# A hybrid of attention, state-space layer and routed experts: the state-space part one step later, taps and decay sums in odd steps, the mask folded into the decay product

## The chip, the cores and the metric

The kernel runs on one core of a Trainium2 chip. The metric is the device time of one execution in microseconds. A core has TensorE (PE; PEld is its weight load), VectorE (DVE), ScalarE (ACT), GpSimd (POOL) and SyncE (SP, here only DMAs). Each engine takes its instructions strictly in the order in which they are written and waits for semaphores in between.

## The reference, cut to what matters

Input x is (8, 32, 32, 128), so 8 images of 1024 tokens with 128 channels.

```python
q = (x * dw1) @ pw1 + b1;  v = (x * dw2) @ pw2 + b2       # per image, 1024 tokens
a = softmax(q @ q.T) @ v * gamma + x                       # attention, no scaling
t = a
n = layernorm(t); xn = rmsnorm(n) * norm_w
z, xBC, dt = split(xn @ W_in.T)                            # 256, 320, 8
xBC = silu(causal_conv4(xBC) + conv_b)                     # four taps
xs, B, C = split(xBC);  dt = softplus(dt + dt_bias)
state = state * exp(-dt * exp(A_log)) + (dt * xs) outer B  # along the tokens, 8 heads of 32, 32 states
y = C . state + Dp * xs
y = rmsnorm(y * silu(z)) * gnorm_w
t = t + n + y @ W_out.T
m = layernorm(t); p = top2(softmax(m @ router_w.T))        # 8 experts, gates sum to 1
out = t + sum over the two of gate * (silu(m @ w1.T) * (m @ w3.T)) @ w2.T   # hidden size 341
```

## The kernel before, in words

The 8192 tokens are 64 tiles of 128. A batch is 8 tiles, one image. `batches` calls `step(base, i)` 79 times; `base` is the batch's first tile and i runs from 0 to 7. The calls are unrolled, and each engine has its own `step` with an order written out by hand. What a step holds:

- tile base+i: its scores against the whole image (TensorE L339 to L341, into pX), their row maximum NM (VectorE L976) and their exponential PR (ScalarE L610). Q is kept as a high and a low part, QH and QL, so that three products of a fast type give full precision.
- tile o = i-1: PR is transposed (L329, into pY), copied to PT (ScalarE L579), multiplied with V (L423, into pa), and TA = product x 1/sum x gamma + X (VectorE L1050).
- every second step, for two tiles at once: the norms of TA (GpSimd L845 to L851), XN and its transposes (odd steps, tiles i-3 and i-2, "front a"), the products for z, dt, x, B and C. In even steps ("front b", tiles i-4 and i-3) VectorE does SZ (L981), softplus of dt (dts, L985 to L1030, a chain of small instructions) and the other three taps of the convolution (`conv`, L950, nine instructions). The first term is ScalarE's CV (L643, three activations).
- tile k = i-LAG, LAG = 5: the state-space part. In odd steps, for two tiles ("decays"), VectorE makes SX (L955) out of Tanh of the taps (TH, ScalarE L663), reads the running sums of dt x A out of bank pc (CT), and splits them into three bf16 parts (C3), which TensorE transposes (L372) and ScalarE copies to CT3 and NCT3. Each tile has its transposes of SX (L378, L379), the exponents of the decay between every two tokens, in pY (L390, L391, L393), their exponential ED (ScalarE L622), M = ED x GT (VectorE L1041), XDT (L1009), XW (GpSimd L811), and the new state ST (L1098).
- tile e = i-LAG-1: y of the tile (L362, L366, into pc), Y2 (VectorE L997 or L999), YG = Y2 x silu(z) (GpSimd L805), its transposes (L403), the output product (L428), and T2 (VectorE L1056).

The exponent product adds three terms per pair of tokens: `later`, a 128x128 bf16 matrix with -1e30 where a token would look ahead (L390), minus the sum at one token (L391) and plus the sum at the other (L393).

At batch ends there is more. In step 7 TensorE makes the Q of the next batch (`project_q`), and in step 0 V (`project_v`), to which GpSimd adds b2 (L855). For the batch before: GpSimd computes the experts' norm at the end of step 5 (L773 to L777), ScalarE the normalised rows XA in step 6 (L653), TensorE their transposes and the logits through bank pd in step 7 (L306, L312). For the batch before that, VectorE runs `route_a` (softmax, best two, one-hot) in step 1 and `route_b` (a row's place in its expert's list) in the middle of step 3, and GpSimd scatters 16 blocks of rows to DRAM in steps 3 to 7 (L858). Behind the last step comes a table of which expert each block of 128 rows belongs to. Then 136 such blocks go through the experts (L496 to L524, L867), and the results are added to T2 and stored.

Two orders matter for the change. ScalarE, even step:

```python
A(TZ[:, j, :], (pb, pd)[j][:, 0:DI], ACT.Tanh)   # L595, twice
A(dts[:, 2], dts[:, 1], ACT.Exp)                 # L597
A(BNAT[:], pa[:, 2 * P:3 * P], ACT.Copy)         # L603, then GT, PR, SQ, YT, XNT, ED
```

VectorE, even step: three taps, NM, SZ and dts, Y2, two of the softplus chain, XDT, the rest of the chain with three taps in between, AD, M, TA, T2, three taps, CT, YO, ST.

## Time and profile before

| | |
|---|---|
| median of 3 runs | 1317.82 us (1317.07 to 1322.14) |
| the profiled execution | 1313.46 us, of which the span is 1311.5 us |
| TensorE busy | 1128.5 us, 86% of the span |
| VectorE | 908.1 us, 69% |
| ScalarE | 689.1 us, 53% |
| GpSimd | 603.7 us, 46% |
| attention with the state-space part | from 16 to some 895 us of the span |
| end of routing, table, last scatters | to 950 us |
| experts | to 1263 us |
| sum and store | to 1311.5 us |

An engine's busy time is the sum of its instructions' time without overlap. Matmul ends are modelled, so neighbouring ones overlap on paper; the distance from start to start tells what one costs.

### The profile page before, as it was taken

What the parts mean: (1) busy time and instruction counts of PE and PEld (TensorE: products, weight loads), DVE (VectorE), ACT (ScalarE), POOL (GpSimd) and SP (SyncE); (2) the same over time, 40 slices, a digit from 0 to 9 for tenths busy, and PEclk for the clock granted to TensorE, in tenths of its full rate; (3) what the DMA queues carried; (4) which work ended last, traced back from release to release, by engine and by line L of the source; (5) the groups of instructions that cost most, each with busy time, mean ns of one, the idle gap of its engine ahead of it and who ended that gap; (6) DMA issues with size and microseconds to landing.
All of it is one profiled execution on the core that took longest, in us unless ns stands there. A gap on an engine that the chain in (4) does not pass through costs nothing. (4 is left out here: it accounts for less than half of the span.)

```text
span 1311.5 us, 28238 instructions
## 1 busy us (share of the span) xinstructions
PE 1128.5 (86%) x7681; PEld 949.8 (72%) x7745; DVE 908.1 (69%) x3041; ACT 689.1 (53%) x1748; POOL 603.7 (46%) x846
## 2 busy tenths in 40 slices
PE   4799999999999999899999999873099999999950
PEld 3688888788778878788878877752078888888740
DVE  2578778978987987987997988672445555555534
ACT  2565676576666666566657656532034444444420
POOL 5133333483475375466458347435434444444420
PEclk9899999999999999999999999886599999999985
DMA  6000000010010010010010100000112222222249
GB/s 180 26 1 9 25 2 9 20 35 14 5 46 17 1 44 16 9 40 20 9 36 22 27 8 20 10 5 29 53 51 58 58 58 57 58 58 58 56 112 301
DMA packets 73029, 54.66 MB, mean 42 GB/s; under 512 B 9781, under 2 KB 67677, under 8 KB 72925
## 3 DMA queue, kind: packets, MB, share of 16 engines
q1 hardware_dynamic: 55437, 31.62, 9.0%
q0 software_dynamic: 8448, 17.45, 4.0%
q10 hardware_dynamic: 9040, 4.33, 1.1%
q8 instruction: 50, 0.82, 0.3%
q14 instruction: 54, 0.44, 0.1%
HBM read 30.67 MB, written 22.69 MB: 41 GB/s over the span
## 5 line engine op out<-in xcount | busy, mean ns | idle before, releaser
L867 POOL DMA_INDIRECT results_by_choice<-YE,DIX x136 | 130.6, 960 | 190.3 <-ACT YE L698 181.1
L858 POOL DMA_INDIRECT rows_by_expert<-XA,SL x128 | 139.2, 1088 | 63.9 <-issue 31.9
L1176 DVE COPY V<-pc 128x384 f32<-128x384 f32 x136 | 75.9, 558 | 132.7 <-PE pc L516 132.7
L362 PEld LDWEIGHTS pc<-XDT,M 128*128 128x128 f32 x1024 | 125.3, 196 | 35.6 <-issue 30.3
L362 PE MATMUL pc<-XDT,M 128*128 128x64 f32 x1024 | 126.4, 278 | 23.1 <-DVE CT L1081 10.5
L950 DVE SCALAR_TENSOR_TENSOR CV<-XBC,cw,CV 128x256 f32<-128x256 f32 x288 | 131.2, 490 | 9.8 <-ACT CV L643 3.2
L423 PE MATMUL pa<-V,PT 128*128 128x128 f32 x1024 | 126.8, 277 | 2.2 <-POOL V L855 0.9
L423 PEld LDWEIGHTS pa<-V,PT 128*128 128x128 f32 x1024 | 119.4, 192 | 6.6 <-issue 6.3
L507 PE MATMUL pX<-W,TA 128*128 x272 | 104.3, 464 | 1.0 <-ACT TA L685 0.7
L509 PE MATMUL pY<-W,TA 128*128 x272 | 101.1, 454 | 0.0
L1041 DVE TENSOR_TENSOR M<-ED,GT 128x1024 f32<-128x1024 f32 x64 | 78.3, 1224 | 32.8 <-ACT ED L622 32.8
L805 POOL TENSOR_TENSOR YG<-Y,SZ 128x256 f32<-128x256 f32 x64 | 46.6, 727 | 108.1 <-DVE Y L997 97.5
L1172 DVE TENSOR_TENSOR X<-XT,pY 128x341 f32<-128x341 f32 x136 | 69.5, 511 | 31.5 <-PE pY L509 19.5
L796 POOL TENSOR_TENSOR STE<-ST,ETOT 32x256 f32<-32x256 f32 x56 | 46.6, 831 | 91.9 <-DVE ST L1098 87.8
L976 DVE TENSOR_REDUCE NM<-pX 128x1 f32<-128x1024 f32 x64 | 77.8, 1216 | 14.3 <-PE pX L341 14.1
L663 ACT ACTIVATE TH<-CV 128x768 f32<-128x768 f32 x32 | 27.0, 844 | 114.8 <-issue 101.8
L685 ACT ACTIVATE TA<-pa 128x128 f32<-128x128 f32 x136 | 37.8, 278 | 79.6 <-PE pa L496 78.7
L610 ACT ACTIVATE PR<-pX,NM 128x1024 f32<-128x1024 f32 x64 | 71.3, 1115 | 9.4 <-DVE NM L976 9.4
L329 PE MATMUL pY<-ident,PR 128*128 128x128 f32 x512 | 68.2, 277 | 3.5 <-ACT XBC L638 2.7
L516 PE MATMUL pc<-ident,X 128*128 128x128 f32 (+1 forms) x408 | 66.9, 273 | 0.0
L524 PEld LDWEIGHTS pb<-W,V 128*128 128x128 f32 (+1 forms) x408 | 56.1, 191 | 14.0 <-issue 1.1
L329 PEld LDWEIGHTS pY<-ident,PR 128*128 128x128 f32 x512 | 57.9, 146 | 11.5 <-issue 10.5
(252 smaller groups left out, 3023.0 us busy)
## 6 DMA issues: line engine op xcount, KB each, us to landing
GX<-rows_by_expert SPq DMA_DIRECT2D x136, 65.0 KB
XT<-in_xT_dram SPq DMA_DIRECT2D x8, 512.0 KB, 3.9
X<-in_x_dram SPq DMA_DIRECT2D x16, 256.0 KB, 3.0
W<-results_by_choice SPq DMA_DIRECT2D x8, 512.0 KB, 8.6
out_dram<-T ACTq DMA_DIRECT2D x8, 512.0 KB, 6.8
results_by_choice<-YE,DIX POOLq DMA_INDIRECT x136, 2.2
rows_by_expert<-XA,SL POOLq DMA_INDIRECT x128
W<-in_w1T_dram SPq DMA_DIRECT2D x1, 1364.0 KB
```

What stands on the lines that cost most here:

```text
L329: last = nc.tensor.transpose(pY[:, P * j:P * j + P], PR[:, P * j:P * j + P], ident[:])
L362: mm(pc[:, 64 * h:64 * h + 64], M[:, h, :], XDT[:, e % 2, HD * h:HD * h + 64], start=h == 0, stop=False, skip_group_check=True)
L423: last = mm(pa[:, 0:C], PT[:, P * j:P * j + P], V[:, j, :], start=j == 0, stop=j == NT - 1)
L507: mm(pX[:, 512 * par:512 * par + HID], GXT[:, par, :], W1[:, cols], start=True, stop=True).then_inc(s("h1_ps"), 1)
L509: mm(pY[:, 512 * par:512 * par + HID], GXT[:, par, :], W3[:, cols], start=True, stop=True).then_inc(s("h3_ps"), 1)
L610: A(PR[:], pX[:], ACT.Exp, bias=NM[:, i:i + 1], accum_out=RS[:, i:i + 1]).then_inc(s("exp_ready"), 1)
L858: g.indirect_dma_start(xg, bass.IndirectOffsetOnAxis(ap=SL[:, j // NT, j % NT:j % NT + 1], axis=0), XA[:, j // NT, j % NT, :], None).then_ ...
L867: g.indirect_dma_start(yg, bass.IndirectOffsetOnAxis(ap=DIX[:, j, :], axis=0), YE[:, j, :], None).then_inc(s(f"ye{j}_scattered"), 16)
L950: return stt(CV[:, m, :], XBC[:, m, fo + tap:fo + tap + 256], cw[:, m, tap:tap + 1], CV[:, m, :], ALU.mult, ALU.add)
L976: v.tensor_reduce(NM[:, i:i + 1], pX[:], AX.X, ALU.max, negate=True).then_inc(s("nm_ready"), 1)
L1041: tt(M[:], ED[:], GT[:, None, :].broadcast_to([P, H, P]), ALU.mult).then_inc(s("m_ready"), 1)
L1176: v.tensor_copy(HT[:, par].rearrange("p k t -> p (k t)"), pc[:, 0:P * len(HC)]).then_inc(s("hT_ready"), 1)
```

## The change

The state-space part runs a step later (LAG 6), while the decay sums stay at i-5 (called d now) and are applied, with the taps, in odd steps. SX and CTP move to the start of the even steps. SZ gets a third buffer.

The mask goes into the product with NCT3. Rows 64 to 127 of NCT3 hold -1e30 where a token would look ahead, once for each half of the tokens, and `pickm` picks them:

```diff
-  mm(pY[:, q], identb[:], later[:, None, :].broadcast_to([P, 4, P]), start=True, stop=False, ...)
-  mm(pY[:, q], NCT3[:, par, :], pick[:, half * H + 4 * h2:half * H + 4 * h2 + 4, :], start=False, ...)
+  four = pY[:, 512 * h2:512 * h2 + 512].rearrange("p (h t) -> p h t", h=4)
+  for th in range(2):
+      mm(four[:, :, HP * th:HP * th + HP], NCT3[:, par, th, :], pickm[:, half * H + 4 * h2:half * H + 4 * h2 + 4, :], start=th == 0, ...)
```

VectorE's `step`, cut to its order (i even: SX; i odd: decay sums and taps):

```diff
-                if decays:
-                    stt(SX...)                      # needs TH
-                    v.tensor_copy(C3[:, 0], CUM) ... # the C3 chain
-                if front_b:
-                    conv(2, 0); conv(2, 1); conv(2, 2)
+                if i % 2 == 0 and there(base, k):
+                    upto(dve, "th_ready", base, k + 2)
+                    stt(SX...)
+                if decays:
+                    upto(dve, "cum_ps", base, d + 2)
+                    tt(CT..., pc[:, 0:4 * H]..., hrow[:, 1:2, :]..., ALU.mult)   # CT = sums x -A
+                    upto(dve, "cv_evac", base, d + 2)
+                    conv(2, 0)
+                    ... C3 chain with conv(2, 1) and conv(2, 2) in between
                 if there(base, i):
                     v.tensor_reduce(NM...)
+                if i == 1 and routes:
+                    routing[base] = route_a(base)
+                    route_on()                      # softmax of the logits, up to PB / sum
...
                 Y2, recip and two small ones of softplus (three now)
                 XDT
+                if decays:
+                    conv(1, 0); conv(1, 1); conv(1, 2)
-                if i == 1 and there(base, -2 * NT): route_a(base)
-                if i == 3 and there(base, -2 * NT): route_b(base)
                 softplus chain, RG            # no taps in between any more
+                if i in (1, 2) and routes: route_on()
+                if decays:
+                    conv(0, 0); conv(0, 1); conv(0, 2)    # then conv_ready
                 M, TA, T2, the two statistics
+                if i in (2, 4) and there(base, NT): take_ql(base + NT, [i // 4])
                 YO, ST
+                if i in (1, 2) and routes: route_on()
+                if i == 2 and routes: PCT copy
+                if i == 3 and routes: route_b(base)
+                if i == 0 and routes: logits copy, maximum, subtraction
```

`route_a` is a generator now, in four parts: softmax; maxima; indices and one-hots; gates. The first two parts and the third run in step 1 (ahead of Y2, ahead of the last three taps, at the end), the fourth in step 2.

ScalarE, even step: TR of two tiles and PT first, then CTP, the two TZ, and now CV ahead of the exponential of dts; in step 0 four of the batch's normalised rows (`normed(base, 1)`) behind it:

```diff
                 if front_b:
                     ... TZ, twice
+                    for m in range(3):
+                        last = A(CV[:, m, :], XBC[:, m, fo:fo + 256], ACT.Identity, bias=cb[:, m:m + 1], scale=cw[:, m, 3:4])
+                    last.then_inc(s("cv_evac"), 2)
                     A(dts[:, 2], dts[:, 1], ACT.Exp).then_inc(s("enau_ready"), 2)
+                if routes:
+                    normed(base, 1)
```

ScalarE, odd step: the exponential of the logits (i = 1) behind XN; TH behind ED and ahead of the two XBC copies, where it stood at the end of the even step. The first four normalised rows come at the end of step 7 (they were eight, in step 6).

TensorE: `project_q` one half in step 2 and one in step 4 into a second buffer of QH and QL, where it was whole in step 7; transposes of the normalised rows and the logits in step 0 of the next batch, in bank pc (`rows_of_x(base, 0)` behind L403, `rows_of_x(base, 1)` behind `project_v`, `logits` behind the state products), where they were in step 7 in bank pd; logits 8 columns wide instead of 64; the sums of dt (not of dt x A) over 16 columns instead of 64.

GpSimd: V isn't biased; b2 x gamma is added to X instead, a half in step 7 and a half in step 3 (`bias_x`, 128x512 each). The experts' norm moves from the end of step 5 to the end of step 6, behind that step's four scatters and norm chain. Its setup builds `pickm` and the masked NCT3, and ScalarE waits for them before its first step.

SyncE: the padding rows go to a DRAM tensor early and from there to their places, the loads of x wait for constants. ZT shares XA's memory. V, the expert stage and the table aren't changed.

## Rows read from the trace of the kernel before

**Rows 1.** Busy time by stretch: from:to, length, each engine's busy time, clock, DMA.

```profile
89.90:192.30 102.40, 97.89 (x720) 85.13 (x727) 80.08 (x248) 68.31 (x167) 37.26 (x68) 1.00 0.04 12
812.70:895.00 82.30, 63.48 (x415) 52.98 (x418) 55.36 (x207) 35.28 (x94) 38.34 (x57) 0.88 0.04 12
```

**Rows 2.** The same for steps 0, 2 and 4 to 7 of one batch: PE, PEld, DVE, ACT, POOL.

```profile
405.54:418.49 12.95, 12.90 (x102) 11.81 (x102) 11.79 (x38) 7.48 (x16) 2.77 (x5) 1.00 0.01 2
...
431.54:444.40 12.86, 12.04 (x89) 10.38 (x90) 12.00 (x39) 7.35 (x16) 3.73 (x5) 1.00 0.01 3
...
457.25:469.96 12.71, 11.68 (x85) 9.90 (x86) 11.49 (x38) 6.58 (x15) 7.94 (x10) 1.00 0.06 18
469.96:482.69 12.73, 11.66 (x85) 9.71 (x86) 9.03 (x27) 8.69 (x24) 8.96 (x14) 1.00 0.24 84
482.69:494.49 11.80, 11.22 (x85) 9.95 (x86) 10.88 (x35) 9.01 (x22) 10.00 (x13) 1.00 0.05 18
494.49:511.53 17.04, 16.12 (x115) 13.52 (x116) 11.58 (x34) 11.65 (x30) 12.81 (x17) 1.00 0.07 25
```

**Rows 3.** TensorE in order of time, steps 4 to 6: start, length, instruction, wait.

```profile
465.14 0.44 PE L403 MATMUL pb<-ident,YG 128*128 128x128 f32 x2 [0.42 <-POOL YG L805]
465.67 2.02 PE L423 MATMUL pa<-V,PT 128*128 128x128 f32 x16
...
469.47 0.43 PE L480 MATMUL pc<-AD,tri 128*128 128x64 f32 x2 [0.46 <-DVE AD L1036]
...
477.87 0.39 PE L403 MATMUL pb<-ident,YG 128*128 128x128 f32 x2
...
482.69 1.06 PE L329 MATMUL pY<-ident,PR 128*128 128x128 f32 x8 [0.25 <-ACT XBC L638]
...
488.66 0.81 PE L390 MATMUL pY<-later,identb 128*128 128x512 bf16 x2
...
489.52 0.61 PE L393 MATMUL pY<-CT,pick 128*128 128x128 bf16 x8
```

**Rows 4.** ScalarE in order of time, steps 4 and 5.

```profile
457.13 1.59 ACT L643 ACTIVATE CV<-XBC,cb,cw 128x256 f32<-128x256 f32 x3
...
460.66 0.39 ACT L595 ACTIVATE TZ<-pd 128x256 f32<-128x256 f32 x1
...
463.36 0.22 ACT L597 ACTIVATE dts<-dts 128x16 f32<-128x16 f32 x1 [2.32 <-DVE dts L985]
...
472.56 0.84 ACT L663 ACTIVATE TH<-CV 128x768 f32<-128x768 f32 x1 [5.65 <-issue]
...
474.61 0.41 ACT L573 ACTIVATE CTP<-SX 32x256 f32<-32x256 f32 x1 [1.00 <-DVE SX L955]
...
476.39 0.88 ACT L589 ACTIVATE XN<-TA,st 128x128 f32<-128x128 f32 x2
```

**Rows 5.** VectorE in order of time, step 4.

```profile
463.85 0.43 DVE L997 TENSOR_TENSOR Y<-pc,YO 128x256 f32<-128x256 f32 x1
```

**Rows 6.** GpSimd in order of time, step 6.

```profile
483.90 1.34 POOL L773 TENSOR_SCALAR rs<-MV 128x8 f32<-128x8 f32 x1 [0.16 <-issue]
...
488.81 0.73 POOL L805 TENSOR_TENSOR YG<-Y,SZ 128x256 f32<-128x256 f32 x1 [0.49 <-DVE Y L999]
...
500.31 0.20 POOL L851 TENSOR_TENSOR st<-st 128x4 f32<-128x4 f32 x1
```

**Rows 7.** VectorE in order of time, first and last part of `route_b`.

```profile
918.95 1.57 DVE L926 TENSOR_TENSOR OFF<-OFF,PCT 128x8 f32<-128x8 f32 x8
...
922.58 0.17 DVE L933 CAST SL<-SLF 128x16 uint32<-128x16 f32 x1 [0.24 <-DVE SLF L932]
```

**Rows 8.** VectorE and GpSimd in order of time, a tap and XW.

```profile
385.00 0.94 DVE L950 SCALAR_TENSOR_TENSOR CV<-XBC,cw,CV 128x256 f32<-128x256 f32 x1
385.02 0.63 POOL L811 TENSOR_TENSOR XW<-XDT,DEC 128x256 f32<-128x256 f32 x1
```

**Rows 9.** The page's costliest groups: count, busy us, mean ns, idle before.

```profile
L950 DVE SCALAR_TENSOR_TENSOR CV<-XBC,cw,CV 128x256 f32<-128x256 f32 x288 | 131.2, 490 | 9.8 <-ACT CV L643 3.2
```

More of the change, by code:

```diff
@@ L729, in _ @@
             g.memset(cb[:], 0.0).then_inc(s("zeroed"), 1)
[L730 to L731 removed]
+            for t, v in ((wx[:, DI + 2 * NS:], 0.0), (CTP[:], 0.0), (XBC[:, :, 0:TAPS - 1], 0.0), (CT3[:], 0.0),
+                         (ST[:], 0.0), (XDT[:, :, DI:], 0.0), (ones[:], 1.0), (mhalf[:], -0.5)):
                 g.memset(t, v)
             g.memset(tri[:], 1.0)
[L734 removed]
             g.memset(pick[:], 0.0).then_inc(s("filled"), 1)
@@ L833, in step @@
                 scatters(3)
-                if i == 5 and there(base, -NT) and not last_norm:
-                    norm_for_experts(base)
                 if i % 2 == 0 and there(base, fn):
@@ L1004, in step @@
                     steps.then(tt(dts[:, 5], dts[:, 2], dts[:, 9], ALU.mult))
+                    steps.then(tt(dts[:, 6], dts[:, 5], dts[:, 5], ALU.mult))
                 if there(base, k):
@@ L1034, in step @@
                 if front_b:
-                    upto(dve, "cum_ps", base, fb)
-                    stt(AD[:, 0:16].rearrange("p (a b) -> p a b", a=2), DT[:, fpar], -1.0, hrow[:, 1:2, :].broadcast_to([P, 2, H]), ALU.mult, ALU.mult).then_inc(s("ad_ready"), 2)
+                    steps.then(stt(DT[:, fpar], dts[:, 7], 2.0, dts[:, 3], ALU.mult, ALU.add), True)
+                    v.nop().then_inc(s("dt_ready"), 2)
+                if i in (1, 2) and routes:
+                    route_on()
+                if decays:
+                    upto(dve, "conv_tap1", base, d + 2)
+                    for m in range(3):
+                        last = conv(0, m)
+                    last.then_inc(s("conv_ready"), 2)
                 if there(base, k):
```

441 lines of the change are left out of this document (222 added, 219 removed).

## The prediction

> **What bounds the kernel now.** I read the page first, then busy time by stretch, then one batch step by step, then one even and one odd step on each engine. In the long stretches [rows 1] the reader is to see TensorE busy for about 96% of a batch at full granted clock (1.00), and VectorE 85% beside it. The eight steps of one batch last 511.53 - 405.54 = 105.99 us [rows 2]. Every step but the last takes 11.8 to 13.05 us (step 1 from the ends of its neighbours); the last takes 17.04, because the Q product and the router's transposes and logits stand in it. So the attention stage is TensorE's, with a few small waits: 0.42 us for YG, 0.46 for AD, 0.25 for the XBC copy [rows 3]. VectorE is busy 9.0 to 12.0 us of each step shown [rows 2]; it has the least room in the even ones. Whatever makes a TensorE instruction wait lengthens the step at once, since each engine runs in its written order and TensorE has nothing in hand to catch up with.
>
> **Work removed from TensorE.** The decay mask was two bf16 products of 512 columns with `later` beside two with `pick`: 489.52 - 488.66 = 0.86 us for the four [rows 3]. Now four products of 256 columns do both, at the same rate 0.43 us. That is 0.43 saved per tile, 3.4 us per batch and 27.5 us over 64 tiles. The narrower decay sums and logits save nothing that I count: they keep their number of weight loads. The Q product (two products, 1.72 us) moves from step 7 into steps 2 and 4, and transposes with logits (about 2.6 us) from step 7 to the next step 0; together they are the 4.3 us by which step 7 exceeds step 5 [rows 2]. Both only move.
>
> **Even steps.** ScalarE now makes the taps' first term CV (three activations, 1.59 us) between the second TZ and the exponential of dts [rows 4]. The second TZ starts 460.66 - 457.25 = 3.4 us into the step, so that exponential starts at 3.4 + 0.4 + 1.5 = 5.3 (now 6.1, held there by VectorE). From it to Y2 are 463.85 - 463.36 = 0.5, and from Y2 to the transposes of YG (L403) 465.14 - 463.85 = 1.3 [rows 3 to 5]: L403 at 7.1. By its own order TensorE would be there at 489.52 - 482.69 = 6.8, plus about 0.45 for the products with CT3, less 0.43: 6.85. L423 waits for XDT, which stands 465.67 - 463.85 = 1.8 behind Y2, and 0.2 more for the square of dts put ahead of it: 7.9. Behind L423 come 469.96 - 465.67 - 0.46 = 3.8 us (the wait for AD goes, as the taps leave the even step). An undisturbed even step is 11.7 us, against 11.80 for step 6. The 0.43 saved is spent waiting for YG and XDT.
>
> **Odd steps.** They gain the nine tap instructions on VectorE (131.2 / 288 = 0.46 us each, 4.1 us [rows 9]) and lose SX (1.0, the wait of CTP [rows 4]). Of step 5 TensorE is idle 12.73 - 11.66 = 1.07 us [rows 2]; most of that is the wait of L362 for CT, about 0.7, and it goes. Its work is 11.66 - 0.43 = 11.2 us. But Tanh of the taps (TH, 0.84 [rows 4]) now needs the last tap and stands on ScalarE ahead of the two XBC copies, and the next step's first transposes already wait for the second of these [rows 3]. L403 of an odd step is at 477.87 - 469.96 = 7.9 today [rows 3], less 0.7 and 0.43: 6.8. XDT starts about there, six taps and two small instructions (3.2) end near 10.1, TH 11.0, the copies 11.9: I take 12.0 us. A clean pair is then 23.7 us, against 24.5 for steps 5 and 6.
>
> Taps against GpSimd: one tap took 0.94 us, where the mean is 0.49, when XW started beside it [rows 8, 9]. Between 0 and 0.5 us per odd step come from that; 0.1 is in the 12.0. The Trainium skill (SBUF — State Buffer, "Who interferes with whom") has it that a VectorE instruction with two SBUF inputs and a GpSimd instruction that reads SBUF shut each other out for a whole instruction. By that rule every odd step, with three taps right behind XDT just as XW is released, pays up to the whole 0.5; the sum would be some 14 us higher. The row agrees that it happens, not how often.
>
> **What the new order does to the routing steps** (six batches route in the attention loop, two behind it).
> Step 1: four small router instructions stand on VectorE ahead of Y2 and wait for ScalarE's exponential of the logits, behind XN. XN stood at 476.39 - 469.96 = 6.4, now some 0.7 earlier; with 0.9 for XN, 0.3 for PB and 1.0 for the four, Y2 is at 7.9, L403 at 9.2, where TensorE would be at 6.8. With the 482.69 - 477.87 = 4.8 us from L403 to the end of an odd step: 14.0.
> Step 2: the maxima's indices and one-hots (some 2 us) run behind step 1 on VectorE, which then is 3.2 us late; SX, CTP, TZ, CV, dts, Y2 follow one on another: L423 at 9.3, plus 3.8, 0.86 and 0.4 for the places: 14.3.
> Step 3: 12.0. Its router block of 922.75 - 918.95 = 3.8 us [rows 7] now stands at the very end, ahead of step 4's SX. VectorE is 5.2 late: SX to CTP 1.0, CTP 0.35, two TZ 0.9, CV 1.5 (the exponential starts near 8.8), then 0.5 and 1.3: L403 near 10.6 instead of 6.85, L423 11.2. Step 4, with its half of Q: 11.2 + 3.8 + 0.9 = 15.9.
> Steps 5 and 6: 12.0 and 11.7.
> Step 7: GpSimd normalises for the experts at the end of step 6, behind four scatters and the norm chain. Today that norm chain ends 500.51 - 488.81 = 11.7 us behind the start of YG of step 6. The experts' chain with STE takes 488.81 - 0.49 - 483.90 = 4.4, of which some 1.1 is its first instruction held up (1.34 instead of about 0.2) [rows 6]: 3.3. YG of step 6 starts at 6.4, so step 7's can't start before 6.4 + 11.7 + 3.3 - 11.7 = 9.7, where 5.2 would do. L403 at 10.4, plus 4.8: 15.2; I take 15.0.
> Step 0: 11.7, V 1.8, transposes and logits 2.6, and 0.4 because ScalarE enters late (it normalises four tiles at the end of step 7, four here): 16.5.
> Sum 16.5 + 14.0 + 14.3 + 12.0 + 15.9 + 12.0 + 11.7 + 15.0 = 111.4 us, against 105.99: 5.4 more. Waits worked out like these partly cover each other, so I take 4.9, 29 us over six batches.
>
> **The rest.** Batch 1 routes nothing: four pairs, Q and V (3.5) and 1.7 in step 7 make 99.5 against 102.40 [rows 1]: -3. Batch 0 holds one state-space tile less and needs no biased V (about -7), while Q's halves sit in steps of only 5 us (+2): -5. Behind attention one more state-space step is needed, 7 to 12 us; the 82.30 us there [rows 1] stand mostly for VectorE, which is better spread, and the experts' norm no longer waits for a scatter: between -4 and +9, I take +3. V's bias on X costs GpSimd 2.4 us per batch as before, hidden in steps 7 and 3. The zero rows go by a DRAM tensor; their eight DMAs stay beside 16 scatters: 0, at most 3. The expert stage isn't touched.
> Sum: 29 - 3 - 5 + 3 = +24 us on the profiled execution's 1313.46. Its span was 1311.5, so 2 us lie around it; the median of the runs shown is 4.4 above it. 1317.8 + 24 = 1342; I say 1340.
>
> **Rivals.**
> (a) TensorE stays the bound (faster). The lags on VectorE and GpSimd are absorbed, because the taps' removal leaves even steps slack: this decides if step 4's L403 starts before 8 us and step 7's before 7.5. Then a batch is 105.99 - 3.4 = 102.6, today's waits included; six batches -20, with the rest -5: 1293. For it: steps now run with VectorE 3 us late and hardly stall. Against it: the instructions between were few; now SX, CV and Y2 form one row.
> (b) Only one of the two long waits comes (step 4 or step 7), about 3 us less per batch: 1321, within the noise. For it: GpSimd's scatters vary from 1.0 to 2.1 us.
> (c) The change doesn't remove what it says: the mask saving is eaten as above but no wait is added: 106 per batch, near 1314.
>
> **How the numbers follow.** Forecast 0.58, (a) 0.28, (b) and (c) 0.14 together. About 0.5% is what a measurement of this kernel can tell from no change. Faster 0.29, same 0.13, slower 0.58. Forecast alone: 1326 to 1360 (the open taps' term, and waits that cover each other). The whole range, which takes in most of (a): 1288 to 1358.
>
> **What would show it.** L403's waits for YG in steps 1, 4 and 7 of over 2 us each; VectorE starting SX of step 4 some 5 us into it; norm for experts ending 6 us or more into step 7; L390 gone and L391's four products near 0.43 us; no wait for AD or CT. If step 4 lasts under 13.5 us and step 7 under 13, I am wrong and the kernel is faster.

## The result, and the profile after

The changed kernel takes 1380.22 us (median of 4 runs, 1375.06 to 1383.37) against 1317.44 us before: ratio 1.0467, 95% interval [1.0425, 1.0509]. It is slower, as forecast, but by 63 us where 24 were forecast, and above the whole range of 1288 to 1358. Its profiled execution took 1379.51 us with a span of 1377.7 us, 66.2 us more than before's 1311.5.

Steps here begin at the first transposes of PR. One routing batch of the kernel after, steps 0 to 7, in the columns of [rows 2] (last: granted clock, DMA share, GB/s):

```profile
421.72:437.62 15.90, 15.57 (x126) 14.40 (x126) 11.69 (x34) 12.19 (x29) 7.70 (x14) 1.00 0.17 58
437.62:454.35 16.73, 14.55 (x88) 13.13 (x88) 11.62 (x43) 8.27 (x22) 2.74 (x5) 0.80 0.00 1
454.35:468.12 13.77, 12.27 (x92) 10.86 (x92) 12.07 (x55) 8.87 (x20) 2.71 (x5) 1.00 0.01 2
468.12:480.23 12.11, 11.81 (x89) 10.30 (x88) 10.84 (x32) 7.99 (x22) 5.62 (x11) 1.00 0.01 1
480.23:498.33 18.10, 13.71 (x88) 11.82 (x88) 15.24 (x51) 8.29 (x19) 9.84 (x11) 0.91 0.10 31
498.33:510.20 11.87, 11.51 (x89) 10.22 (x88) 10.33 (x29) 7.76 (x21) 8.98 (x15) 1.00 0.05 18
510.20:521.06 10.86, 10.55 (x83) 9.66 (x84) 8.99 (x29) 7.63 (x18) 4.34 (x7) 1.00 0.06 21
521.06:539.48 18.42, 14.46 (x89) 12.93 (x88) 12.18 (x34) 8.24 (x21) 15.81 (x23) 0.81 0.07 23
```

The reader is to see three things. Undisturbed steps (5 and 6) are shorter than before, together 22.73 us against 24.53 [rows 2]. Steps 1, 4 and 7 are long, and TensorE is idle in them for 2.2 to 4.4 us. And just these three have a granted clock under 1.00 (1.00 is 2.4 GHz, 0.50 is 1.2). The idle time is the forecast wait for YG at its transposes (L405, before L403), TensorE in order of time:

```profile
447.83 0.33 PE L405 MATMUL pb<-ident,YG 128*128 128x128 f32 x1 [2.18 <-POOL YG L823]
...
491.54 0.33 PE L405 MATMUL pb<-ident,YG 128*128 128x128 f32 x1 [3.52 <-POOL YG L823]
...
531.71 0.48 PE L405 MATMUL pb<-ident,YG 128*128 128x128 f32 x1 [3.73 <-POOL YG L823]
```

Against [rows 3], where the wait was 0.42 us. What the forecast did not have is in finer windows of steps 4 and 7:

```profile
490.00:492.00 2.00, 0.44 (x2) 0.20 (x2) 1.90 (x7) 1.93 (x7) 0.95 (x2) 1.00 0.00 0
492.00:494.00 2.00, 1.72 (x13) 1.75 (x14) 1.81 (x9) 1.31 (x3) 1.58 (x2) 0.84 0.03 8
494.00:496.00 2.00, 2.00 (x10) 2.00 (x10) 1.50 (x3) 0.00 (x0) 1.72 (x3) 0.50 0.11 33
...
532.00:534.00 2.00, 2.00 (x11) 2.00 (x10) 1.09 (x2) 1.66 (x5) 1.80 (x3) 0.50 0.11 33
534.00:536.00 2.00, 2.00 (x11) 2.00 (x11) 1.23 (x1) 0.95 (x2) 1.84 (x3) 0.50 0.10 33
```

Behind the wait TensorE is busy all the time, but at 0.50. The sixteen products of L425 in step 4 take 2.76 us (2.02 in [rows 3]):

```profile
492.29 2.76 PE L425 MATMUL pa<-V,PT 128*128 128x128 f32 x16 [0.31 <-issue]
```

The same wait does not always do it. Of the 18 waits in steps 1, 4 and 7 of the six routing batches, 17 have such a stretch behind them. The one without is in step 4 of batch 6 (counted from 0), where TensorE waited 3.23 us; that step lasted 16.2 us, where the five others lasted 17.8 to 18.7:

```profile
712.42:728.59 16.17, 12.07 (x88) 10.47 (x88) 14.61 (x49) 8.29 (x19) 8.49 (x10) 1.00 0.04 13
```

And some such stretches stand behind no wait. In step 1 of two batches, this one included, the clock is at 0.50 from 1.1 us into the step, before the wait for YG, although TensorE had been busy without a break (V's products, the router's transposes, sixteen products of 8 columns):

```profile
430.00:437.62 7.62, 7.62 (x64) 7.29 (x65) 4.61 (x16) 3.97 (x9) 3.45 (x10) 1.00 0.30 104
438.80:442.20 3.40, 3.40 (x13) 2.91 (x12) 2.87 (x11) 1.45 (x4) 0.00 (x0) 0.50 0.00 0
```

These two steps lasted 16.7 us, the four others 15.1. What brings this stretch no run here isolates.

Over the whole kernel, L425 (L423 before), L405's wait and the taps, against [rows 9]; the tap's mean rose from 490 to 555 ns, 18 us in all:

```profile
L425 PE MATMUL pa<-V,PT 128*128 128x128 f32 x1024 | 151.8, 310 | 11.6 <-issue 5.9
...
L978 DVE SCALAR_TENSOR_TENSOR CV<-XBC,cw,CV 128x256 f32<-128x256 f32 x288 | 149.6, 555 | 0.3
...
L405 PE MATMUL pb<-ident,YG 128*128 128x128 f32 x128 | 30.5, 324 | 72.8 <-POOL YG L823 72.4
```

The folded mask is as priced, 516.60 - 516.16 = 0.44 us for its four products:

```profile
516.16 0.60 PE L393 MATMUL pY<-pickm,NCT 128*128 128x256 bf16 x4
516.60 0.28 PE L395 MATMUL pY<-CT,pick 128*128 128x128 bf16 x2
```

Where the 66.2 us stand, from the starts of the steps in both traces, each batch from its step 0 to its step 7 as in the forecast: the first PR transposes start at 28.64 us instead of 25.53 (+3.1); batch 0 -3.9; batch 1 -3.5 (98.8 us against 102.2); the six routing batches +58.5 (692.6 against 634.1); from the last PR transposes to the end +11.9 (495.4 against 483.5).

### The profile page after: what moved, and what is told of

Its sections match the earlier page's. It is cut to its first block and busy times, and to the rows that moved or that the text cites. A ratio compares the mean times of both kernels' runs of the same rounds, so it can differ in the third digit from the quotient of the medians.

```text
span 1377.7 us, 28282 instructions
## 1 busy us (share of the span) xinstructions
PE 1149.1 (83%) x7744; PEld 992.9 (72%) x7745; DVE 931.0 (68%) x3003; ACT 693.8 (50%) x1748; POOL 598.5 (43%) x858
## 5 line engine op out<-in xcount | busy, mean ns | idle before, releaser
L425 PE MATMUL pa<-V,PT 128*128 128x128 f32 x1024 | 151.8, 310 | 11.6 <-issue 5.9
L425 PEld LDWEIGHTS pa<-V,PT 128*128 128x128 f32 x1024 | 142.0, 222 | 21.9 <-issue 21.6
L978 DVE SCALAR_TENSOR_TENSOR CV<-XBC,cw,CV 128x256 f32<-128x256 f32 x288 | 149.6, 555 | 0.3
L405 PE MATMUL pb<-ident,YG 128*128 128x128 f32 x128 | 30.5, 324 | 72.8 <-POOL YG L823 72.4
L405 PEld LDWEIGHTS pb<-ident,YG 128*128 128x128 f32 x128 | 14.0, 153 | 81.1 <-POOL YG L823 80.9
L584 ACT ACTIVATE PT<-pY 128x1024 f32<-128x1024 f32 x64 | 65.0, 1016 | 13.5 <-PE pY L326 12.9
L326 PEld LDWEIGHTS pY<-ident,PR 128*128 128x128 f32 x512 | 58.0, 147 | 17.9 <-issue 16.9
L814 POOL TENSOR_TENSOR STE<-ST,ETOT 32x256 f32<-32x256 f32 x56 | 41.4, 739 | 60.1 <-DVE ST L1116 60.0
```

What stands on the lines that cost most here:

```text
L326: last = nc.tensor.transpose(pY[:, P * j:P * j + P], PR[:, P * j:P * j + P], ident[:])
L425: last = mm(pa[:, 0:C], PT[:, P * j:P * j + P], V[:, j, :], start=j == 0, stop=j == NT - 1)
L978: return stt(CV[:, m, :], XBC[:, m, fo + tap:fo + tap + 256], cw[:, m, tap:tap + 1], CV[:, m, :], ALU.mult, ALU.add)
```

## The experiments

All times are medians, each ratio against the kernel before measured beside it; "the six routing batches" below are the 47 steps from the first step 1 to the last step 7, 621.2 us before and 676.7 after; "batch" is the mean of five of them, each from its step 1 to the next step 0, 105.8 us before and 115.8 after; "tail" is what lies behind the last PR transposes, 483.5 and 495.4 us.

**1. The experts' norm out of YG's way.** GpSimd's order after it: YG, XW, RY of step 7, then the norm.

```diff
-                if i == 6 and there(base, -NT):
+                if i == 7 and there(base, -NT):      # behind RY
                     norm_for_experts(base)
```

> Edit: in the changed kernel the experts' norm on GpSimd stands in step 7, behind RY, instead of at the end of step 6. Theory A (three waits for YG, and each also brings a spell at half granted clock): step 7 falls from 18.4 to about 12.5 us, because its wait of 3.7 us goes and so does the half clock behind it; six batches give 35 us, 1345 us. Theory B (the waits alone cost, the clock is unrelated): the wait goes but the step keeps slow products: 3.5 us per batch, 1359 us. Theory C (four scatters per step on GpSimd hold YG back whatever the norm does): step 7 stays above 16 us, 1370 us or more.

Measured: 1379.92 us, ratio 1.0499 [1.0479, 1.0518]: no gain. But step 7 did what theory A says, and step 0 paid. Its steps 7 and 0:

```profile
630.99:644.32 13.33, 11.82 (x88) 10.18 (x88) 10.77 (x31) 7.85 (x20) 11.67 (x17) 1.00 0.07 22
644.32:663.02 18.70, 16.06 (x125) 14.36 (x126) 11.70 (x38) 12.46 (x29) 11.16 (x19) 1.00 0.14 50
```

18.2 fell to 13.3, 15.9 rose to 18.7 (ScalarE's normalising, which waits for the norm, now stands ahead of step 0's work), and the tail grew by 6.8 us. Two things here bear on the clock: behind step 0's new wait for YG of 2.06 us it stayed at 1.00 in four of six batches, and step 1, with its wait of 2.18 us as before, lasted 14.0 us in three batches, where the clock stayed at 1.00, and 16.7 in the three others.

**2. The second router block on GpSimd.**

```diff
-                if i == 3 and routes:                 # VectorE, end of step 3
-                    route_b(base)
                 scatters(2)
                 if i == 3 and there(base, -2 * NT):
+                    route_b(base)                     # GpSimd, ahead of the scatters
```

> Edit: in the changed kernel the router's second block (running sums, slots) runs on GpSimd in step 3, where that engine idles some 8 us, instead of on VectorE at the end of step 3; the sums over eight experts are three additions each there. Theory A: VectorE starts SX of step 4 some 3.6 us sooner, the wait of 3.5 us for YG and the half clock behind it go, step 4 falls from 18.1 to about 12.5 us: 33 us, near 1347 us. Theory B (waits alone): 3.5 us per batch, 1359 us. Theory C (the bias on X and the scatters on GpSimd, beside VectorE's small instructions of step 4, are what is late, not the router block): step 4 stays above 15.5 us, 1365 us or more.

Measured: 1385.41 us, 1.0532 [1.0512, 1.0552]; step 4 still 18.2 us: theory C. In step 4 of one batch, VectorE and then GpSimd:

```profile
486.29 0.42 DVE L1034 TENSOR_TENSOR Y<-pc,YO 128x256 f32<-128x256 f32 x1
```
```profile
486.85 1.08 POOL L896 DMA_INDIRECT rows_by_expert<-XA,SL  x1 [0.85 <-POOL SL L888]
488.24 0.96 POOL L896 DMA_INDIRECT rows_by_expert<-XA,SL  x1 [0.30 <-issue]
489.22 1.27 POOL L893 TENSOR_TENSOR X<-X,b2b 128x512 f32<-128x512 f32 x1
490.44 0.65 POOL L814 TENSOR_TENSOR STE<-ST,ETOT 32x256 f32<-32x256 f32 x1
491.05 0.71 POOL L823 TENSOR_TENSOR YG<-Y,SZ 128x256 f32<-128x256 f32 x1
```

Y2 starts 5.7 us into the step, over 4 us sooner than in the changed kernel (490.26 - 480.23 = 10.0), and YG starts just as late, behind two scatters, the bias and STE. But the move did not leave GpSimd's queue as it was. The block takes 8.2 us there (477.85 to 486.00) where VectorE needed 3.7, and the scatters, which wait for its slots, start 6.3 us into the step instead of 5.8. So the run shows that GpSimd's row of work behind the slots is as long as VectorE's, and not that it would be late without the block. In the changed kernel the two end 0.5 us apart: STE at 490.23, Y2 at 490.68. And VectorE's part has a piece of GpSimd's in it. The exponential of dts waited, long behind CV, for a small instruction that lasted 1.86 us beside the bias addition (488.39 to 489.66):

```profile
487.84 1.86 DVE L1021 SCALAR_TENSOR_TENSOR dts<-dts 128x16 f32<-128x16 f32 x1
```
```profile
489.80 0.21 ACT L614 ACTIVATE dts<-dts 128x16 f32<-128x16 f32 x1 [1.36 <-DVE dts L1021]
```

**3. The softmax behind XDT and the taps.**

```diff
-                    route_on()            # step 1, ahead of Y2
+                if i == 1 and routes:     # behind the three conv(1, m)
+                    route_on()
```

> Edit: in the changed kernel the first part of the router's block in step 1 (four small instructions that wait for the exponential of the logits) stands behind XDT and the three taps that follow it, instead of ahead of Y2. Theory A: the wait of 2.2 us for YG in step 1 and the half clock behind it (products at about 4 us instead of 2) go, some of it comes back because the last taps are later: 3.5 us per batch, 1359 us. Theory B (waits alone): 1.5 to 2 us per batch, 1369 us. Theory C (the lateness only moves into step 2, which already waits 1.2 us for YG): 1378 to 1385 us.

Measured: 1373.92 us, 1.0451 [1.0433, 1.0468]. Step 1 is 13.8 us in every batch (15.1 or 16.7 in the changed kernel), L405 at 6.3 instead of 8.6 or 10.2; step 2 stays at 13.85. A batch is 2.1 us shorter: A had 3.5, B 1.5 to 2, and the median is nearer to B's as well. The ratios of this kernel and the changed one (1.0451 and 1.0467) can't be told apart; the steps can. They also say what the 2.1 us were: with the wait kept and the clock at 1.00, step 1 lasts 14.0 us (experiments 1 and 4), so here the wait itself was worth 0.2 us and the rest is the clock's, as theory A has it.

**4. The waits kept, TensorE busy in them.**

```diff
+                    if 2 * NT <= base < TILES:
+                        for _ in range({1: 7, 4: 13, 7: 13}.get(i, 0)):
+                            nc.tensor.transpose(pb[:, 0:P], ident[:], ident[:])
                     upto(pe, "yg_ready", base, e + 1)
```

> Edit: in the changed kernel TensorE makes 7, 13 and 13 transposes of the identity matrix, whose result nobody reads, just ahead of the wait for YG in steps 1, 4 and 7 of the six batches with routing; they last a little less than those waits, which stay. Theory A (the half granted clock follows from TensorE's idling in these waits): the granted clock stays at 1.00 behind the waits, L425 lasts 2.0 us there instead of 2.8 to 3.6, and some 7.5 us per batch come back: 45 us, 1335 us. Theory B (the clock is lowered for another reason, or its spells cost nothing because others end the step): 1375 to 1385 us. If the transposes outlast the waits the kernel gets slower by their excess.

Measured: 1359.16 us, 1.0325 [1.0302, 1.0349]. One such transpose takes 0.122 us, less than I had counted with, so in step 7 TensorE still idled for 2.3 us, and in four of six batches the clock still fell there (17.2 us, 15.5 in the two others); in step 4, with 1.8 to 2.2 us left, it fell in two. Hence a second one, with 17, 27 and 28:

> Edit: as busy_while_waiting, with 17, 27 and 28 transposes instead of 7, 13 and 13, since one took 0.122 us (13 in 1.59 us) and TensorE still idled for over 2 us ahead of YG in step 7, where the granted clock still fell to 0.50. Theory A: no stretch at 0.50 in steps 1, 4 and 7; step 7 falls from 17.2 to 15.6, step 4 stays at 16.2: 8 us less than the 1359 us of busy_while_waiting, about 1350 us. If a transposes' row outlasts its wait, up to 1 us per batch comes back. Rival: the clock falls although TensorE is busy: 1359 us or more.

Measured: 1356.13 us, 1.0330 [1.0309, 1.0351]. Its steps 1, 4 and 7:

```profile
428.42:442.44 14.02, 13.36 (x106) 12.03 (x105) 11.20 (x42) 8.15 (x22) 2.73 (x5) 1.00 0.01 4
...
468.39:484.86 16.47, 15.02 (x115) 13.36 (x115) 14.59 (x49) 8.30 (x19) 8.53 (x10) 1.00 0.04 14
...
508.07:523.61 15.54, 14.64 (x116) 13.17 (x116) 11.99 (x34) 8.12 (x21) 13.25 (x21) 1.00 0.06 18
```

Nothing reads these transposes, YG comes as late as before them (L405 10.65 us into step 7 in both kernels), and yet the three steps fall from 16.73, 18.10 and 18.42 us to 14.0, 16.5 and 15.5, at clock 1.00. It is so in 17 of the 18 steps. In step 1 of the last batch (15.6 us) the clock was at 0.50 from 0.5 us into the step, ahead of the wait, as in the two long steps 1 of the result. The six routing batches take 649.2 us instead of 676.7: the half clock cost 27.5 us in these two traced executions. By the medians it is 24.1 us and by the ratios (1.0467 and 1.0330) some 18, since both kernels' times spread over 5 to 8 us; the two fillings can't be told apart by their ratios at all (1.0325 and 1.0330), only by their steps. The time that is left, 28.0 us above before, is the waits less what the undisturbed steps gain.

**5. The same wait in the kernel before.** ScalarE starts a copy of YG to DRAM; TensorE's transposes wait for it too, in steps 4 and 7.

```diff
                     upto(act, "yg_ready", base, e + 1)
+                    if i in (4, 7) and 2 * NT <= base < TILES:
+                        act.dma_start(hold, YG[:]).then_inc(s("held"), 16)
```

> Edit: the kernel before with one thing added: in steps 4 and 7 of the six routing batches TensorE waits, ahead of its transposes of YG, also for a DMA of 128 KB that ScalarE starts once YG is ready and whose copy nobody reads. No engine gets more work than twelve DMA issues. The DMA should hold TensorE for some 3 us more (its length is read from the trace). Theory A (an idle TensorE is followed by a spell at half granted clock, whatever the kernel): the steps grow by more than the wait, by 1.5 to 2.5 us each; with waits of 3 us 12 x 5 = 60 us, 1372 us, and stretches at 0.50 behind them. Rival (in the kernel before the clock stays, the half clock in the changed kernel has another reason): 12 x 3 = 36 us less what slack takes, 1350 us or less.

Measured: 1332.66 us, 1.0138 [1.0111, 1.0165]. TensorE in step 4, then the clock there:

```profile
470.57 0.41 PE L406 MATMUL pb<-ident,YG 128*128 128x128 f32 x2 [2.34 <-DMA hold<-YG]
470.82 3.10 PE L426 MATMUL pa<-V,PT 128*128 128x128 f32 x16
```
```profile
470.50:472.00 1.50, 1.43 (x10) 1.43 (x11) 1.02 (x4) 0.98 (x2) 1.20 (x3) 0.84 0.14 44
472.00:474.00 2.00, 2.00 (x11) 2.00 (x11) 1.90 (x8) 0.32 (x1) 1.64 (x2) 0.50 0.12 37
```

So the half clock is no property of the new order: a wait of 2.3 us brings it here as well (3.10 us for the sixteen products, 2.02 in [rows 3]). It does so in four of six batches, where step 4 lasts 15.1 to 15.3 us. In the last one the wait is 2.34 us too, the clock stays at 1.00, and step 4 lasts 13.6: the half clock alone is worth 1.6 us here. In the first one it stays at 1.00 behind 2.71 us. The total is far below theory A's 1372 us, and its bare number would fit the rival: the waits on that DMA were 1.9 us each on the mean (23.2 us for 12), behind those of step 7 (1.5 us) the clock stayed at 1.00, and step 5 gave 1.2 us back.

**6. GpSimd's bias where it idles.** X's two halves get their bias at the start of step 1 and in step 3 ahead of the scatters, not at the ends of steps 7 and 3.

> Edit: in the changed kernel GpSimd adds the bias to X's second half in step 3 ahead of its wait for the slots (it idles there), and to the first half at the start of step 1, instead of at the ends of steps 3 and 7; nothing else moves. The run with the router block on GpSimd showed Y2 of step 4 ready at 486.7 and YG only at 491.05, behind two scatters, the bias (1.27 us) and STE. Theory A (VectorE's lateness sets YG of step 4): at most 0.5 us per batch, 1376 to 1380 us. Theory D (GpSimd's own queue stands as high as VectorE's): the bias held a small VectorE instruction for 1.7 us and GpSimd itself for 1.27 us, so YG of step 4 starts 1.5 to 2 us sooner, with a shorter spell at half clock step 4 falls by 2.5 us; step 0 and 7 by 0.5: some 15 us, 1365 us.

Measured: 1373.93 us, 1.0460 [1.0443, 1.0478]. The ratio is that of the changed kernel (1.0467) within the noise; in the traces the six routing batches are 8.1 us shorter. Step 4 does what theory D says: it falls to 15.0 or 16.6 us, and L405 there stands at 9.85 to 10.2 us instead of 11.0 to 11.4; step 3 grows from 11.9 to 13.0, since the bias now runs beside the taps. There, on VectorE and GpSimd:

```profile
475.02 2.36 DVE L978 SCALAR_TENSOR_TENSOR CV<-XBC,cw,CV 128x256 f32<-128x256 f32 x3
```
```profile
475.43 1.27 POOL L876 TENSOR_TENSOR X<-X,b2b 128x512 f32<-128x512 f32 x1
```

Three taps take 2.36 us instead of 1.4; one of them lasted 1.57. The Trainium skill (SBUF — State Buffer, "Who interferes with whom") says that a VectorE instruction with two SBUF inputs and a GpSimd one that reads SBUF exclude each other for a whole instruction, and the rows agree.

**7. All moves together, and one by one from there.** norm_step7, softmax_behind_xdt, bias_off_queue, and six of `route_b`'s eight sums ahead of XDT in step 3:

> Edit: in the changed kernel four moves together: the experts' norm in step 7 behind RY, the softmax's first part behind XDT in step 1, six of the eight running sums of the second router block ahead of XDT in step 3 (VectorE idles there), the rest at its old place, and both bias additions where GpSimd idles. Steps expected: 0 15.9, 1 13.8, 2 13.8, 3 12.0, 4 14.5, 5 11.9, 6 10.9, 7 13.3, together 106.1 against 117. Theory A with D (three waits, their half clock, and GpSimd's queue): 65 us less in six batches, the tail stays 12 us longer than before: 1315 to 1325 us. Theory C (the moves push the lateness into the next step, as the norm did with step 0): 1345 us or more.

Measured: 1359.98 us, 1.0360 [1.0342, 1.0377]: theory C in the total. Batch 111.9, of which step 0 18.7. Step 4 is 13.8, better than expected; step 3 13.5 and step 0 worse. In half of the batches step 1 lasts 15.4 us instead of 13.8, at half clock from its start, with no wait for YG in it. So ScalarE's eight activations next:

```diff
-                if i == 7 and there(base, -NT): ... normed(base + NT, 0)
                 if routes:
-                    normed(base, 1)
+                    normed(base, 0)
 ...
                 if routes:
+                    normed(base, 1)                   # behind ED
                     rows_of_x(base, 1)
```

> Edit: as all_moved_off, with two more: ScalarE normalises the router's first four tiles in step 0 behind the exponential of dts and the other four behind ED, instead of four at the end of step 7 (where it waits for the norm, which the earlier edit made 5 us later) and four behind the exponential; and ScalarE waits for the masks at its first use of them in step 5 of the first batch, not ahead of the first step. Theory A with D (each engine's queue of small work lies ahead of YG): step 0 falls from 18.7 to 15.9 us, 17 us in six batches, and the first step starts 3 us sooner, as in the kernel before (25.5 instead of 28.6 us into the span): 1340 us. Rival F (step 0 is held by GpSimd's bias and router work on TensorE): only the 3 us, 1357 us.

Measured: 1344.07 us, 1.0222 [1.0187, 1.0256]. Step 0 17.1, batch 109.6. The first step still starts at 28.58: ScalarE's wait for the masks was not what delays it (below). Two variants of this kernel:

> Edit: as norms_in_step0, with the exponential of dts ahead of the taps' first term CV on ScalarE, its order in the kernel before. The prediction priced CV ahead of it at 1.5 us on the path to XDT of every even step, and took an even step at 11.7 us, but clean even steps lasted 10.87. Theory G (where VectorE and ScalarE are on time TensorE still sets the even step): no change in steps 2 and 6, some 1 us in steps 0 and 4, whose YG is late: 5 to 12 us less than norms_in_step0. Theory H (CV late makes the next step's taps late instead): same or up to 5 us more.

Measured: 1354.75 us, 1.0300 [1.0270, 1.0329], 10.7 us more: theory H's direction, beyond its size. Clean even steps 10.76 instead of 10.87 us, step 0 18.3 instead of 17.1 (7.5 us in all), and step 1 has the stretch at half clock in four batches instead of one (4.8 us). CV ahead of the exponential costs 0.1 us in a clean even step, and no more in steps 2 and 4.

> Edit: as norms_in_step0, with both bias additions of GpSimd at the ends of steps 3 and 7, where the changed kernel has them. In bias_off_queue the addition beside the taps cost step 3 1.1 us, while step 4 gained 1.5 to 3. Theory D: step 3 12.3 instead of 13.4, step 4 15.5 instead of 13.8, step 0 a little longer: 5 us more than norms_in_step0. Rival: the two cancel: within 3 us.

Measured: 1361.18 us, 1.0351 [1.0322, 1.0381]: theory D, three times its size: step 4 16.1 to 17.9 us, step 0 18.2, and step 1 at half clock from its start in five of six batches.

Then GpSimd's whole queue was rearranged:

```diff
-            SPREAD = {(4, 1): (2,), (4, 2): (3, 4), (5, 0): (5,), ...
+            SPREAD = {(4, 0): (0,), (4, 1): (1,), (4, 2): (2,), (5, 0): (3,), (5, 1): (4,), (5, 2): (5,),
+                      (6, 0): (6,), (6, 1): (7,), (6, 2): (8,), (7, 0): (9,), (7, 1): (10,), (7, 3): (11,),
+                      (0, 0): (12,), (0, 1): (13,), (0, 2): (14,), (0, 3): (15,)}
+                if i in (1, 2) and there(base, 0) and base > 0:
+                    upto(pool, "s_ready", base, i + 1)
+                    bias_x(base, i - 1)
```

> Edit: norms_in_step0 with GpSimd's queue rearranged: three scatters in each of steps 4 to 7 and four in the next step 0, all behind YG, instead of two at the end of step 3, three, three, four and four; the second router block on GpSimd in step 3; each bias addition beside VectorE's maximum NM, which reads PSUM alone, in steps 1 and 2; the masks built last in the setup. Theory D (GpSimd's queue and the bias beside the taps are what is left): steps 0 15.9, 1 13.8, 2 13.8, 3 12.0, 4 12.5, 5 11.9, 6 10.9, 7 12.5, together 103.3 against 109.3 in norms_in_step0 and 106.0 before; the first step starts at 25.6 again: 36 + 3 us less than norms_in_step0: 1305 us. Theory J (VectorE, 93 us busy per batch in the changed kernel, or the tail, sets the time whatever the queues do): 1325 us or more.

Measured: 1322.14 us (9 runs), 1.0052 [1.0035, 1.0069]. One batch, steps 0 to 7:

```profile
396.54:412.96 16.42, 15.73 (x125) 14.44 (x126) 11.13 (x37) 12.32 (x29) 12.35 (x17) 1.00 0.19 68
412.96:426.75 13.79, 11.51 (x88) 10.25 (x88) 12.20 (x42) 7.90 (x22) 5.00 (x9) 1.00 0.01 3
426.75:442.93 16.18, 13.81 (x91) 12.36 (x92) 14.00 (x60) 8.95 (x20) 4.89 (x10) 0.89 0.00 1
442.93:454.82 11.89, 11.52 (x88) 10.23 (x88) 10.01 (x30) 7.98 (x22) 7.66 (x14) 1.00 0.01 2
454.82:466.98 12.16, 11.84 (x87) 10.43 (x88) 9.76 (x31) 8.32 (x19) 10.03 (x22) 1.00 0.04 12
466.98:479.50 12.52, 11.75 (x88) 10.24 (x88) 10.70 (x33) 7.75 (x21) 9.98 (x15) 1.00 0.12 38
479.50:490.36 10.86, 10.54 (x83) 9.67 (x84) 9.09 (x29) 7.64 (x18) 4.34 (x7) 1.00 0.06 20
490.36:502.97 12.61, 11.80 (x88) 10.18 (x88) 10.95 (x33) 7.74 (x21) 11.16 (x17) 1.00 0.06 18
```

The total lies between theory D's 1305 us and J's 1325. Steps 4 and 7 are down from 18.1 and 18.4 us to 12.2 and 12.6; the first step still starts at 28.65 us, and step 2, expected at 13.8, has a wait for YG of 2.1 us and lasts 14.8 us, 16.2 in the two batches in which the clock falls. Four moves were made at once here, and only the block's place is taken apart below. The batch is 105.7 us, 10.1 less than in the changed kernel and level with before; the last PR transposes start 9.5 us earlier than before's (818.6 against 828.1). Only the tail, 501.0 us, keeps it behind. With the router block left on VectorE:

> Edit: as scatters_spread, but the second router block stays on VectorE, in two parts in step 3 as in norms_in_step0. Theory D: VectorE is 2.3 us late into step 4, its YG with it: 1 to 2 us per batch more than scatters_spread, 1312 to 1318 us. If VectorE is the bound (theory J) the difference is the block's whole length, 3.6 us per batch: 20 us more.

Measured: 1336.62 us, 1.0159 [1.0134, 1.0185]; batch 109.0. The difference is 3.3 us per batch, nearly the block's 3.6, but that is no proof of theory J. Of the 20.9 us by which the six routing batches are longer, 11.5 stand in step 4 (13.8 instead of 12.2 us, theory D's size), and 6.4 in step 1, which has the stretch at half clock from its start in four batches instead of none. The tail is 495.2 us against 501.0: the last scatter stands 129.4 us behind the last PR transposes, 134.4 with the block on GpSimd. So the move that shortens the batches is also what lengthens the tail.

**8. The tail.** In scatters_spread, transposes into the idle bank pX, eight ahead of each of four waits per step, sixty ahead of the router's last transposes:

> Edit: scatters_spread, with transposes of the identity into the idle bank pX, which nobody reads, behind the attention stage only: eight ahead of each of four waits of a state-space step, sixty ahead of the router's last transposes. There the granted clock lay between 0.50 and 0.84 in most stretches, and the state-space steps came 10 to 13 us apart. Theory A (the half clock makes the tail's steps long): the seven steps shrink by 1.5 to 2 us each: 12 us less, 1310 us. Theory K (the chain through VectorE, ScalarE and GpSimd sets them): within 3 us of 1322 us, or some us slower, as 32 transposes per step take 4 us of TensorE's time.

Measured: 1323.66 us, 1.0058 [1.0038, 1.0078]: theory K. The granted clock is 1.00 in seven of the first eight stretches of 10 us (0.50 to 1.00 in scatters_spread), and the tail is as long (502.1 us). Two of them:

```profile
849.00:859.00 10.00, 7.97 (x66) 6.72 (x64) 7.87 (x39) 5.72 (x16) 1.33 (x2) 1.00 0.01 2
...
879.00:889.00 10.00, 7.20 (x33) 6.34 (x33) 2.67 (x6) 1.81 (x4) 6.89 (x12) 0.66 0.06 21
```
With fourteen more in step 2:

> Edit: tail_filled, and fourteen such transposes into pb ahead of the wait for YG in step 2 of the six routing batches, where scatters_spread idles 2.06 us and in two of five batches then runs at half clock for a while (16.2 instead of 14.7 us). Theory A: those two or three batches get 1.5 us each back: 3 to 4 us less than tail_filled, about 1307 us, which would beat the kernel before (1314.6 us). Rival: the transposes only delay YG's: no gain.

Measured: 1322.25 us (8 runs), 1.0047 [1.0031, 1.0063], no gain. Step 2 is 14.7 or 14.8 us in the full batches, as expected, but in two batches step 1 now takes the 1.6 us instead, at half clock from 0.5 us into the step, with no wait of over 1 us in the 9 us before. So filling a wait took away the half clock behind it, and not half clock altogether. In the kernel before:

> Edit: the kernel before with the same eight transposes ahead of each of four waits in the steps behind its attention stage; nothing else. Theory A: its tail, whose granted clock was 0.66 to 0.82 in four of its first five stretches of 10 us, has one step less to gain from: 6 to 10 us less, 1306 us. Theory K: within 3 us of 1314.6 us.

Measured: 1312.32 us (12 runs), 0.9978 [0.9967, 0.9989], 0.2% less: theory K again. The clock was at 1.00 in the first six stretches of 10 us behind the last PR transposes (0.61 to 1.00 before), and the tail took 484.7 us against 483.5; the traced execution is shorter only because its first PR transposes start 1.6 us earlier. No version with the new order beats the kernel before.

**9. The mask alone, in the kernel before.**

```diff
-    mm(pY[:, q], identb[:], later[:, None, :].broadcast_to([P, 4, P]), start=True, ...)
-    mm(pY[:, q], NCT3[:, par, :], pick[:, ...], start=False, ...)
+    for th in range(2):
+        mm(four[:, :, HP * th:HP * th + HP], NCT3[:, par, th, :], pickm[:, ...], start=th == 0, ...)
```

> Edit: the kernel before with the folded mask alone (four products of 256 columns with the mask inside, instead of four of 512); its order stays. By the prediction's 0.43 us per tile 27.5 us less if TensorE's length is what counts: 1288 us. If VectorE and GpSimd take over as the bound in some steps (L403's position behind YG), about half: 1300 us. Theory E (the fold gives nothing because TensorE then waits): 1312 to 1316 us.

> Edit: the kernel before with the folded mask, and ScalarE's wait for the masks at its first use of them in step 5 instead of ahead of the first step. mask_alone started its first step 3.1 us later (28.65 against 25.53 us) and gave nothing in the steps: 106.6 against 106.0 us in the batch at 420 us, although L403 stood 0.37 us earlier. Theory E (a TensorE product less gives nothing, because the next wait is as long): 1313 to 1318 us, no change from before. Theory I (mask_alone hid a gain behind the late start): 1305 us or less.

Measured: 1321.14 us, 1.0058 [1.0041, 1.0075], and 1320.61 us (10 runs), 1.0038 [1.0018, 1.0059]. In both the batch is 106.1 us, in both L403 stands 0.37 us earlier in a clean step of batch 1 (6.90 instead of 7.27), and the step is as long as before (11.32 us): theory E in the steps. The totals lie 5 and 3 us above the ends of its ranges: the start is 3 us late, and the tail takes 3 us more than before (486.3 and 486.9 against 483.5), for which no run here gives the reason. The late start is GpSimd's: it builds the masks ahead of clearing ZT, which now falls beside VectorE's setup (mask_late_wait, VectorE and GpSimd):

```profile
19.21 2.67 DVE L1143 TENSOR_SCALAR cw<-cw 128x12 f32<-128x12 f32 x1
```
```profile
20.02 1.82 POOL L768 MEMSET ZT<- 128x2080 f32 x1
```

A scaling of 12 columns lasts 2.67 us and ends with the memset. It accounts for some 1.6 us; the other 1.3 lie in the later start of TensorE's first product. In scatters_spread the masks are built behind the memset, the scaling takes 1.11 us beside them, two more of VectorE's small setup instructions take 1.1 us each, and the first step starts at 28.65 all the same. So it is GpSimd's longer setup beside VectorE's that costs, whichever part of it comes last.

## Why the prediction was wrong

**Its mechanism stood, step by step.** At full granted clock (busy_to_the_end) the steps 1, 2, 3, 4 and 7 lasted 14.0, 13.85, 11.9, 16.2 to 16.5 and 15.5 us, where the forecast had 14.0, 14.3, 12.0, 15.9 and 15.0. Step 0 took 15.9 (16.5), steps 5 and 6 12.36 and 10.87 (12.0 and 11.7). L405 stood at 8.6, 11.0 to 11.4 and 10.65 us in steps 1, 4 and 7, forecast 9.2, 10.6 and 10.4. The six routing batches from step 0 to step 7 cost 31.0 us more than before; the forecast was 29.

**The step that failed is "what the new order does to the routing steps": a wait was priced as its own length.** I noted the full granted clock of the first stretch of [rows 1] and never asked what becomes of it when TensorE idles for 2 to 4 us, though the second stretch there, with TensorE busy for 77%, stands at 0.88. The term was put at nothing. The runs show it: 27.5 us in the changed kernel's trace, 1.6 of them perhaps of the kind that stands behind no wait; gone when TensorE is kept busy, and met again when the kernel before is made to wait. 24 + 27.5 = 51.5 of 66. The Trainium skill (TensorE: Matmul & The Clock Gate, "HAM oscillation — how this bites in real kernels") tells of a kernel in which TensorE falls back to half rate behind every wait for a DMA of 3 to 5 us. The trace agrees for most of such waits and not for all (3.23 us in step 4 of batch 6), and shows it behind 2.18 us as well. Two of the three waits that I forecast myself were of that length (L403 3.8 us late in step 4, 3.6 in step 7).

**The remaining 15 us.** "Behind attention +3" was 11.9. The last YG stands 79.2 us behind the last PR transposes instead of 62.7, so the state-space step more cost 16.5 us and not 7 to 12; 3.8 of them came back by the last scatter (129.4 against 116.7). The chain through all engines sets it, not the clock (tail_filled). "Batch 0: -5" was -0.8: -3.9 came, and the setup, which I had not priced, took 3.1. "Batch 1: -3" was -3.5 (its own terms add up to 100.0, not 99.5; it took 98.8). The routing batches make the other 2.

**Step 4's cause was half the story.** I named VectorE's lateness, and SX did start 4.6 us into the step (5 forecast). But the 1.5 us of CV that I counted on the way to Y2 were not on it: the exponential of dts waited 1.4 us longer than CV took, for an instruction held up beside GpSimd's bias. And GpSimd's scatters, bias and STE, released by the same router block, ended within 0.5 us of Y2. That L405 came so near to 10.6 is in part luck. Moving the bias alone brought it 1.2 us forward (bias_off_queue), moving the block to GpSimd nothing. Step 7's cause was named rightly, but the norm's removal alone only moved the time on into step 0.

**The undisturbed even step** was right up to L425: L405 at 7.0 us (7.1 forecast), L425 at 7.8 (7.9). Step 6 was still 0.8 us shorter than forecast, because what stands behind L425 took 3.1 us and not 3.8: 0.43 is a product that this step does not have (L463, which the first state-space tile of an image leaves out; that tile's step moved from 5 to 6), and 0.13 the narrower decay sums (0.36 us instead of 0.49), which I had counted as no gain. **The mask** was right: four products for 0.44 us, and nothing gained. **Taps against GpSimd**: 18.4 us more of VectorE's time over 32 odd steps, 0.57 each, a little above the upper bound of 0.5, but hidden: the odd steps still took 11.87. (By that bound the sum would have been 0.4 x 32 = 13 us higher, and it was not.) **The range** was written carelessly: its upper end of 1358 lies below the 1360 of the forecast alone.

## What to carry to other kernels

A wait of TensorE of some 2 us or more, in a stretch where it has been busy throughout, costs its length and then, more often than not, about 1 to 3 us again at half clock; put that second term into every sum, and when a trace shows products of one form at two durations, look at the granted clock first. When a wait is filled or removed, count the stretches at half clock again over all batches: they can turn up in another step, and a total can then agree with a theory by chance. When an instruction is late, read the queues of all engines that feed it: two causes of the same length hide each other. An instruction saved on the busiest engine gains nothing where the next wait is as long.

## What the runs showed of the hardware

- The granted clock fell to 0.50 behind waits of TensorE of 1.84 us (step 1 of mask_late_wait) to 3.73 us, but not behind every one. In the routing batches it fell behind 17 of 18 waits of 2.2 to 3.7 us in the changed kernel, 6 of 12 of 1.8 to 2.3 us in busy_while_waiting, 4 of 6 of 2.3 to 2.7 us and none of 6 of 1.5 us in yg_held_in_before. It stayed at 1.00 behind one of 3.23 us.
- The price of one such stretch, in steps with the same wait: 1.1 us in step 1 (15.1 against 14.0), 1.6 in step 4 of yg_held_in_before, 1.7 to 2.9 in steps 4 and 7 of the changed kernel.
- It also fell at the start of step 1 in some batches with no wait over 1 us in the 9 us before (tail_and_step2_filled, 1.6 us each); no run isolates why.
- Transposes of an identity matrix that nobody reads, 0.122 us each, held the clock at 1.00 through the waits of 17 of 18 steps in busy_to_the_end, and delayed nothing as long as they ended ahead of the wait's end (L405 8.6 us into step 1 and 10.65 into step 7, with them and without).
- An instruction of VectorE on 16 columns (0.17 us) lasted 1.86 us beside GpSimd's bias addition in step 4 of the changed kernel, and a scaling (0.17 us) 2.67 us beside GpSimd's memset of 2080 columns. In scatters_spread the addition did not run beside the maximum NM as meant, but just ahead of it, beside a cast on 16 columns, which took 1.25 us instead of 0.16.
